# First output-head product in three fp32r passes, with GpSimd's early sums of weights moved behind its masks

## What is computed

```
h = relu(layernorm(x))                        # h0
xs = [h]
for W, b in ((W0, b0), (W1, b1), (W2, b2)):   # W is 512 x 256
    m = concatenate([h[dst], h[src] - h[dst]], axis=-1) @ W + b
    h = relu(segment_sum(m, dst) / maximum(count(dst), 1))
    xs.append(h)
x = x + concatenate(xs, axis=-1) @ Wf + bf    # Wf is 1024 x 256
```

## Time and profile before

| | us |
|---|---|
| median of 3 runs | 114.17 (113.99 to 114.22) |
| profiled execution | 114.17 |
| its span in the profile | 112.4 |
| busy: PE, DVE, ACT, POOL | 100.6, 92.5, 57.4, 19.8 |

### The profile page before, as it was taken

The page is one execution under the profiler, slowest core; times in us unless marked ns, Lnnn a source line. Parts: engine busy times, 40 slices in busy tenths (PEclk is TensorE's granted clock), DMA queues, the critical chain, the costliest instruction groups (busy, mean ns, idle before and its releaser), DMA issues.

```text
span 112.4 us, 2688 instructions
## 1 busy us (share of the span) xinstructions
PE 100.6 (89%) x1040; PEld 92.4 (82%) x1040; DVE 92.5 (82%) x266; ACT 57.4 (51%) x143; POOL 19.8 (18%) x27
## 2 busy tenths in 40 slices
PE   0398999799999999999899999998999998999930
PEld 0335898687998899989899999997999997999720
DVE  2399999999999999999986699767989989437950
ACT  2497999997897690312807035506233145141630
POOL 7100000000000099410093700660000000000000
PEclk9999999999999999999999999999999999999997
DMA  1867810000200000000153000000000000000044
GB/s 42 239 207 181 281 34 0 0 6 3 92 7 0 6 9 6 0 0 3 14 172 99 0 0 0 0 6 0 0 6 0 0 0 0 0 0 6 0 109 121
DMA packets 5401, 4.63 MB, mean 41 GB/s; under 512 B 555, under 2 KB 5386, under 8 KB 5386
## 3 DMA queue, kind: packets, MB, share of 16 engines
q1 hardware_dynamic: 4460, 3.68, 11.5%
q10 hardware_dynamic: 926, 0.75, 2.4%
HBM read 3.79 MB, written 0.64 MB: 39 GB/s over the span
## 4 chain that ended last, share of the span: by engine, by line
PE 36%; issue 24%; DVE 21%; ACT 7%; POOL 5%; DMA 3%; DVEq 0%; SPq 0%; POOLq 0%; ACTq 0%
PE bank L1125 8%; PE bank L1127 7%; PE bank L1126 7%; PE bank L1375 7%; DMA edge_rows_i<-in_dst_dram 3%; DVE stats L534 3%; DVE pre L741 3%; DVE x_in L674 2%; POOL parts L480 2%; POOL own L489 2%; PE bank L1415 2%; PE bank L1188 2%; DVE h_lo L751 2%; DVE pre L745 1%; PE bank L1275 1%
## 5 line engine op out<-in xcount | busy, mean ns | idle before, releaser
L581 DVE TENSOR_SCALAR src_hot<-node_id,edge_cols 125x626 f16<-125x626 f16 x77 | 23.5, 380 | 0.0
L1275 PEld LDWEIGHTS bank<-dst_hot,src_hot 125*128 125x128 f16 x505 | 19.0, 98 | 3.3 <-DVE src_hot L581 1.7
L1275 PE MATMUL bank<-dst_hot,src_hot 125*128 125x84 f16 (+6 forms) x505 | 20.4, 195 | 1.4 <-DVE src_hot L581 0.9
L1375 PE MATMUL bank<-counts,u_lo 125*128 125x312 f32 (+1 forms) x60 | 16.3, 308 | 0.0
L1051 ACT ACTIVATE h_hi<-pre 128x312 fp32r<-128x312 f32 (+1 forms) x12 | 5.6, 466 | 18.1 <-DVE pre L745 18.1
L480 POOL TENSOR_TENSOR parts<-parts 125x625 f32<-125x625 f32 x5 | 6.4, 1297 | 43.1 <-DVE src_hot L581 35.9
L1375 PE MATMUL bank<-counts,u_hi 125*128 125x312 f32 (+1 forms) x48 | 14.0, 307 | 0.0
L1375 PEld LDWEIGHTS bank<-counts,u_lo 125*128 125x128 f32 x60 | 10.9, 189 | 0.0
L994 ACT ACTIVATE parts<-bank 125x250 f32<-125x250 f32 x25 | 10.2, 411 | 0.0
L1375 PEld LDWEIGHTS bank<-counts,u_hi 125*128 125x128 f32 x48 | 9.1, 189 | 0.0
L918 ACT ACTIVATE counts<-bank 125x125 fp32r<-125x125 f32 (+1 forms) x25 | 7.4, 297 | 2.0 <-PE bank L1275 2.0
(11 more groups left out here) (143 smaller groups left out, 252.8 us busy)
## 6 DMA issues: line engine op xcount, KB each, us to landing
raw<-in_L_gnn_W_dram SPq DMA_DIRECT2D x3, 512.0 KB, 6.5
x_in<-in_x_dram ACTq DMA_DIRECT2D x1, 560.0 KB
raw<-in_L_gnn_Wf_dram SPq DMA_DIRECT2D x1, 512.0 KB, 3.8
out_dram<-x_in SPq DMA_DIRECT2D x2, 168.0 KB
wf<-in_L_gnn_Wf_dram SPq DMA_DIRECT2D x1, 256.0 KB, 7.8
raw<-in_L_gnn_Wf_dram SPq DMA_DIRECT2D x1, 256.0 KB, 2.8
raw<-in_L_gnn_W_dram SPq DMA_DIRECT2D x1, 256.0 KB, 3.5
out_dram<-x_in SPq DMA_DIRECT2D x2, 112.0 KB
```

What stands on the lines that cost most here:

```text
L581: dve.tensor_scalar(src_hot[:, t % RING, 0:IDS], node_id[:, 0:IDS], edge_cols[:, 0, t:t + 1], None, ALU.is_equal).then_inc(src_hot_vector, 1)
L1275: return pe.matmul(built[s][:, :, n0:n0 + n], src_hot[:, t % RING, BLK * s:BLK * s + P], dst_hot[:, c, :, j // 2, c0:c0 + n, j % 2], start ...
L1375: ins = pe.matmul(bank[KF * h + f][:, 0:e - a], u[:, k, P * f:P * (f + 1)], counts[0:BLK, k, a:e], start=False, stop=(k == NB - 1 and u is ...
```

## The change

`head_0` uses `project`, as the other heads do, on `h0_hi`, `h0_lo`, `wf0_hi`, `wf0_lo`, four new tensors. ScalarE copies the two halves of h0_t (128x625 each) to h0_hi where wf1's high part was made, after row block 3; wf0's and then wf1's high part come after row block 4. GpSimd makes h0_lo (two subtractions) in the place of the sums, and wf0_lo behind the first masks; wf1_lo and the sums of row blocks 0 and 1 come behind the second masks. The counts waited for in `w_hi` and `w_lo_pool` go up by one to match; the transfer of W4 starts on the same event as before. TensorE waits for h0_lo and wf0_lo in front of `head_0` instead of for wf0's transfer. A branch for inputs with unusual edge order, not taken here, zeroes all five row blocks.

```diff
-            for r in EARLY_SUMS:
-                sum_weights(r)
-            low_part(HI_WF1, wf1[1][:, :, :], raw[0][:, 0:KF, :], wf1[0][:, :, :])
+            for f in range(KF):
+                pool.wait_ge(h0_hi_ready, f + 1)
+                pool.tensor_tensor(h0_lo[:, f, 0:NODES], h0_t[:, f, 0:NODES], h0_hi[:, f, 0:NODES].bitcast(F32),
+                                   ALU.subtract).then_inc(h0_lo_ready, 1)
             mask_own_0(0)
+            low_part(HI_WF0, wf0_lo[:, :, :], wf0[:, :, :], wf0_hi[:, :, :])
             pool.wait_ge(block_built, NB * NB)
             pool.memset(weights_hi[:, :, NODES:NODES_E].bitcast(F32), 0.0)
             pool.memset(weights_lo[:, :, NODES:NODES_E].bitcast(F32), 0.0).then_inc(weights_padded, 1)
             mask_own_0(1)
+            low_part(HI_WF1, wf1[1][:, :, :], raw[0][:, 0:KF, :], wf1[0][:, :, :])
+            sum_weights(0)
+            sum_weights(1)
             pool.wait_ge(u_lo_ready, NB + 1)
...
                 if r == 3:
-                    act.wait_ge(raw_loaded[0], 32)
-                    high_part(wf1[0][:, :, :], raw[0][:, 0:KF, :])
-
+                    act.wait_ge(h0_t_ready, NB)
+                    for f in range(KF):
+                        copy(h0_hi[:, f, 0:NODES], h0_t[:, f, 0:NODES]).then_inc(h0_hi_ready, 1)
+
+            act.wait_ge(wf0_loaded, 16)
+            high_part(wf0_hi[:, :, :], wf0[:, :, :])
+            act.wait_ge(raw_loaded[0], 32)
+            high_part(wf1[0][:, :, :], raw[0][:, 0:KF, :])
             act.wait_ge(raw_loaded[2], 16)
             high_part(wb[2][0][:, :, :], raw[2][:, KF:2 * KF, :])
...
             def head_0():
 
-                pe.wait_ge(wf0_loaded, 16)
+                pe.wait_ge(h0_lo_ready, KF)
+                pe.wait_ge(*LO_WF0)
                 for b in range(NB):
-                    o = fill(("head", 0, b))[0:BLK, 0:D]
-                    for k in range(KF):
-                        ins = pe.matmul(o, h0_t[:, k, BLK * b:BLK * (b + 1)], wf0[:, k, :],
-                                        start=(k == 0), stop=(k == KF - 1))
-                    ins.then_inc(filled, 1)
+                    project(("head", 0, b), feature_rows(h0_hi, h0_lo, b),
+                            [(wf0_hi[:, k, :], wf0_lo[:, k, :]) for k in range(KF)])
```

More of the change, by code:

```diff
@@ L233, in gnn_kernel @@
         wf0 = sb("wf0", [P, KF, D], F32)
+        wf0_hi = sb("wf0_hi", [P, KF, D], F32R)
+        wf0_lo = sb("wf0_lo", [P, KF, D], F32R)
+        h0_hi = sb("h0_hi", [P, KF, NODES_E], F32R)
+        h0_lo = sb("h0_lo", [P, KF, NODES_E], F32R)
         wd = [None] + [[sb(f"wd{l}_{s}", [P, KF, D], F32R) for s in ("hi", "lo")] for l in range(1, LAYERS)]
@@ L323, in gnn_kernel @@
         h0_t_ready = sem("h0_t_ready")
+        h0_hi_ready = sem("h0_hi_ready")
+        h0_lo_ready = sem("h0_lo_ready")
         w_diff = sem("w_diff")
@@ L363, in gnn_kernel @@
         COUNT_COLS = ((0, 2 * BLK), (2 * BLK, 4 * BLK), (4 * BLK, NODES_E))
-        EARLY_SUMS = (0, 1)
         U0_BLOCKS = ((0, 1), (2, 3), (4,))
@@ L417, in gnn_kernel @@
                     (raw[1], rows(Wf)[:, 4:8, :], raw_loaded[1], (w_lo_vector, 2)),
[L418 to L423, removed]
+                    (raw[2], rows(W4), raw_loaded[2], (w_lo_pool, 4))]
+        LO_WB = (None, (w_lo_vector, 1), (w_lo_pool, 3))
+        LO_WD = (None, (w_lo_vector, 2), (w_lo_pool, 4))
+        LO_WF0, LO_WF1, LO_WF23, LO_W4 = [(w_lo_pool, n) for n in (1, 2, 5, 6)]
+        HI_WB1, HI_WF0, HI_WF1, HI_WB2, HI_WD1, HI_WD2, HI_WF23, HI_W4 = range(1, 9)
         block = ctx.enter_context(nc.Block())
@@ L683, in _ @@
                 dve.memset(slow_hot[:, IDS:IDS + 1], 1.0)
-                dve.memset(parts[:, len(EARLY_SUMS):NB, :, 1, :], 0.0)
+                dve.memset(parts[:, :, :, 1, :], 0.0)
                 for k in range(2):
@@ L690, in _ @@
                     dve.wait_ge(parts_ready, 2 * k + 2)
-                dve.wait_ge(weights_summed, len(EARLY_SUMS))
                 for r in range(NB):
```

## The result

The changed kernel takes 116.80 us (median of four, 116.38 to 117.09); the kernel before took 114.08 in the same series. The ratio is 1.024, with a 95% interval of 1.022 to 1.027. The prediction was 116.6 us, slower.

What follows compares the result with a forecast made beforehand. VectorE's queue was taken to bound the kernel, its two-operand instructions held by GpSimd's reads: 0.51+0.97+0.47+0.46=2.41 us on its chain, so 114.17+2.41=116.58, forecast 116.6 us, range 115.4 to 117.4.

Steps and rivals of the forecast that it cites:

- What bounds the kernel: VectorE's queue up to `add_head` of block 2 sets the time; TensorE is ahead and waits for it.
- TensorE's passes worth nothing: In `head_0`, thirty passes take 3.7 us for 4.13; the 0.4 saved goes into TensorE's wait for VectorE.
- rival (b): TensorE's saving of 0.4 in `head_0` reaches the end: 113.8 us; 4 in 100.
- ScalarE's copies hidden: Two h0 copies, 1.6 us from 37.50, and wf0's and wf1's high parts after row block 4 fit idle time.
- h0_lo at 1.5 us each: GpSimd's two h0_lo subtractions before the first masks end between 41.9 and 42.4, hold nobody and cost nothing.
- wf0_lo, +0.51: Behind GpSimd's first masks, wf0_lo catches VectorE's L745 at 44.47, which ends at 45.49 instead of 44.98.
- wf1_lo, +0.97: Behind GpSimd's second masks, wf1_lo makes VectorE's wb_lo end at 50.59 instead of 49.62.
- sums, +0.47 and +0.46: Behind wf1_lo, GpSimd's two sums each hold a VectorE L745, ending at 51.97 for 51.50 and 53.35 for 52.89.
- Everything behind moves along: After own terms start at 57.50 for 55.09, all later work shifts equally; 114.17+2.41=116.58 us.
- Rival (c), the clock: TensorE's clock falls to 1.2 GHz in its new waits, slowing u and own terms: about 119 to 121; 5 in 100.
- Rival (a), GpSimd gives way: At the four meetings GpSimd is held behind VectorE instead, price 0, from 48.2 to 53; 10 in 100.
- Rival (d), wf0_lo late: wf0_lo ends over 1.6 us later than reckoned and holds `head_0`: about 116.6 again; 3 in 100.

Runs made afterwards that it cites:

- The head alone: Kernel before with the first head in three passes, high parts standing in for low ones, wf1's high part in its old place: 114.08 us for 114.11, ratio 1.000.
- cutting the existing meetings: Kernel before with GpSimd's masks cut into three by has_edge's columns and wf1's low part moved later: 113.40 us for 114.11, ratio 0.995.
- first head-alone kernel: Kernel before with a three-pass first head, high parts for low ones, ScalarE's copies placed as in the change: 114.64 us, ratio 1.005.
- the memsets: Changed kernel with GpSimd only writing (memsets) in place of wf1's low part and the two early sums: 114.14 us, ratio 1.000.
- the move alone: Kernel before with only wf1's low part and the two early sums put behind GpSimd's second masks, head unchanged: 116.11 us, ratio 1.017.
- the matmuls in the wait: Changed kernel with nine extra matmuls of 512 zero columns on TensorE before its wait for h_lo inside u: 116.31 us, ratio 1.020.

## Why the prediction was right

- *What bounds the kernel.* Right: VectorE's queue up to `add_head` of block 2. The head alone gives 1.000, and cutting the existing meetings gives 0.995.
- *TensorE's passes worth nothing* (against rival (b)). Right, by the head with GpSimd at its old times. `head_0` was 3.55 us for the 3.7 forecast.
- *ScalarE's copies hidden.* Right: the copies of h0 run from 37.48 to 38.91, wb2's ends at 43.35 and h_hi follows at 45.49. The order had a cost that the prediction didn't look for: in the first head-alone kernel a wait of 0.54 us by one GpSimd instruction became a meeting of 0.45.
- *h0_lo at 1.5 us each,* and no one held: right (1.54).
- *wf0_lo, +0.51.* 0.48. Right in place and size.
- *wf1_lo, +0.97; sums, +0.47 and +0.46.* Right in place, short in size: 1.10, 0.58 and 0.58. The term mis-sized is the time by which a caught GpSimd instruction ends after its release. It was taken at 1.03 and 1.04, scaled from a mask; each of the three took 1.15 (wf1_lo 48.99 to 50.14, sums 50.69 to 51.84 and 52.19 to 53.34). Sum 2.74 for 2.41.
- *Everything behind moves along.* Not quite: of the 3.37 us at the start of the own terms 0.7 came back, 0.23 inside them (only where the clock had fallen: in the traces of the memsets, the move alone and the matmuls in the wait nothing comes back there), 0.3 in the last stretch, the rest in small pieces. None of it was foreseen.
- *Rival (c), the clock, 5 in 100.* Too low. By the mean clocks it happened in three of four executions, on top of the meetings, and cost 0.4 to 0.5 us, not the 2.4 to 4.4 reckoned. Part of the time that u took longer lay inside the wait for `add_head`, and the clock was back when the own terms began, so the 3.6 us reckoned for these never came.
- *The number itself is partly luck.* Own terms started at 58.46 for the 57.50 forecast, 0.33 from meetings sized too small and 0.63 from a clock put at nothing; the 0.7 that came back covers most of these 0.96.
- *Rival (a), GpSimd gives way.* Excluded by all four meetings. *Rival (d), wf0_lo late:* it was over at 45.11, long before `head_0` at 46.80.

## What to carry to other kernels

Before work goes to an idle GpSimd, lay its reads beside VectorE's instructions: one that reads two SBUF operands, or a fast fp16 one, stands still until the GpSimd instruction ends, about a microsecond for 512 columns. Where VectorE sets the time it is lost in full (1.07 of 1.07 us); where it doesn't, less (about 0.3 of 1.48). Place such work where VectorE reads from PSUM, or cut it so that it ends before VectorE's next two-operand instruction; moving it on may only move the meeting into the next layer. A shorter product on an engine that waits for another was worth nothing here, not even after the other's queue had been shortened once: the next wait took the saving.

## What the runs showed of the hardware beyond that

Memsets on GpSimd, 3.8 us of them, did not slow two-operand VectorE instructions at all, while one subtraction of 512 columns cost 1.07 us. A one-operand fp16 instruction of 626 columns in 0.38 us was held for 0.75 and 0.78. The Trainium skill, again in "Who interferes with whom", has the second as its case of a 2-port mode; the runs agree.

TensorE's clock fell to 1.2 GHz after an idle time of 2.33 us in the midst of work, and was back at 2.4 GHz about 3.2 us later. By its mean clock it did not fall in one execution out of four of the same kernel.

In all 14 traces a step in the last stretch of the kernel takes 0.55 us where VectorE has the wait for the early sums in the branch that isn't taken, and 0.25 where it hasn't (and the sums stand elsewhere). Who compares two kernels to a tenth of a microsecond should look for such a difference far from the edit.
